# Edge pass of a graph network on one core: TensorE's segment sums move to the end of its step, and ScalarE's and VectorE's steps are put in another order

## The reference

```
gate = silu(edge_attr @ F1W + F1b) @ F2W + F2b          # 40 -> 48 -> 48, per edge
gate = gate + (emb[z[src]] * (emb[z[dst]] @ adapt)).sum(-1)
cw   = where(d < 6, 0.5 * (cos(pi * d / 6) + 1), 0)      # d: the edge's distance
msg  = gate * h[dst] * cw * node_mult[dst]
agg  = segment_sum(msg, src);  tot = segment_sum(node_mult[dst], src)
```

## Time and profile before

| what | before |
|---|---|
| three executions, median | 16926.92 us (16877.77 to 16951.38) |
| profiled execution, first to last instruction (its span; the record has no other time for it) | 19341.2 us |
| busy in it: TensorE, VectorE, GpSimd, ScalarE | 10354.6, 11255.4, 9389.6, 5378.0 us |
| edge pass, from its first transpose to its last eviction | 2577 to 6382 us |

### The profile page before, as it was taken

The page is one execution under the profiler, slowest core; times in us unless marked ns, Lnnn a source line. Parts: engine busy times, 40 slices in busy tenths (PEclk is TensorE's granted clock), DMA queues, the critical chain, the costliest instruction groups (busy, mean ns, idle before and its releaser), DMA issues. The chain is left out here.

```text
span 19341.2 us, 391384 instructions
## 1 busy us (share of the span) xinstructions
PE 10354.6 (54%) x115995; PEld 7977.8 (41%) x115995; DVE 11255.4 (58%) x26413; ACT 5378.0 (28%) x15471; POOL 9389.6 (49%) x11101
## 2 busy tenths in 40 slices
PE   1001046666666326884895787588355555543332
PEld 1001024444444116774784676477233333332332
DVE  6567034444444456885887688588533333347667
ACT  0000012222222003651563465266122222222221
POOL 7788654444444533441441343144254545538466
PEclk9755555555555559997997998799666666675665
DMA  4432334443435316554552754455211111152432
GB/s 130 143 86 64 96 73 73 73 74 73 74 73 72 49 31 226 160 143 141 171 161 63 238 161 124 172 162 161 57 38 45 41 45 41 43 170 60 115 113 49
DMA packets 1458569, 1976.55 MB, mean 102 GB/s; under 512 B 411908, under 2 KB 1125764, under 8 KB 1451465
## 3 DMA queue, kind: packets, MB, share of 16 engines
q1 hardware_dynamic: 1074622, 1326.66, 21.9%
q0 software_dynamic: 309216, 511.82, 14.6%
q10 hardware_dynamic: 74552, 135.95, 2.2%
HBM read 1245.74 MB, written 614.07 MB: 96 GB/s over the span
## 5 line engine op out<-in xcount | busy, mean ns | idle before, releaser
L681 POOL DMA_INDIRECT attend_rows<-key_rows,attend_fetch_now x1824 | 1754.4, 962 | 2354.8 <-PE attend_seg L1717 2026.0
L681 POOL DMA_INDIRECT edges_rows<-raw,edges_perm_now x1824 | 1765.3, 968 | 2006.2 <-issue 1631.5
L1761 ACT ACTIVATE attend_hot<-attend_lane_hot,attend_share 128x128 f32<-128x128 fp8e4 x7296 | 2227.1, 387 | 107.4 <-DVE attend_share L1784 73.5
L681 POOL DMA_INDIRECT mlp_xin<-table,mlp_staged x1564 | 1493.5, 955 | 1440.0 <-PEq L2308 979.9
L681 POOL DMA_INDIRECT keys_rows<-table,keys_staged x1564 | 1869.2, 1195 | 532.9 <-issue 532.9
L1717 PE MATMUL attend_seg<-attend_rows,attend_hot 128*128 128x49 f32 x14592 | 1847.3, 281 | 69.8 <-issue 38.9
L1717 PEld LDWEIGHTS attend_seg<-attend_rows,attend_hot 128*128 128x128 f32 x14592 | 1772.7, 198 | 109.6 <-issue 104.9
L681 POOL DMA_INDIRECT tally_rows<-rows_by_source,tally_origin_now x912 | 1210.9, 1328 | 297.4 <-issue 243.9
L1704 PE MATMUL attend_qx<-attend_table,attend_oht 128*128 128x90 bf16 x21888 | 1108.8, 209 | 445.5 <-DMA attend_oht<-src_hots 395.4
L1704 PEld LDWEIGHTS attend_qx<-attend_table,attend_oht 128*128 128x128 fp8e4 x21888 | 1011.7, 101 | 518.4 <-issue 516.6
L1801 DVE TENSOR_REDUCE attend_mraw<-attend_top 128x2 f32<-128x1024 f32 x912 | 1110.7, 1218 | 60.5 <-issue 30.7
(11 more groups left out here) (543 smaller groups left out, 23684.6 us busy)
## 6 DMA issues: line engine op xcount, KB each, us to landing
key_rows<-expand_out SPq DMA_DIRECT2D x304, 624.0 KB
attend_ea<-edge_attrs SPq DMA_DIRECT2D x912, 160.0 KB
attend_table<-q SPq DMA_DIRECT2D x1832, 67.5 KB
expand_oht<-dst_hots SPq DMA_DIRECT2D x304, 384.0 KB, 3.9
attend_oht<-src_hots SPq DMA_DIRECT2D x912, 128.0 KB
attend_lane_hot<-src_hots_by_edge SPq DMA_DIRECT2D x912, 128.0 KB
raw<-keys_rows ACTq DMA_DIRECT2D x46, 2176.0 KB
rows_by_source<-spread_out SPq DMA_DIRECT2D x152, 576.0 KB, 4.8
```

What stands on the lines that cost most here:

```text
L681: return nc.gpsimd.indirect_dma_start(out=out, out_offset=None, in_=table, in_offset=bass.IndirectOffsetOnAxis(ap=index, axis=0))
L1761: ins = nc.scalar.activation(hot[p][:, u, c, :], lane_hot8[r][:, u, c, :], ACT.Copy, scale=share[p][:, u, c:c + 1])
```

## The change

- TensorE: S moves from second place in the step to the last, behind A. The order becomes T, B, E, A, S.
- `val3` becomes two buffers, used in turn.
- ScalarE: step n now does the tables and the transposed attributes of chunk n-1, then the gate of chunk n-2, then the rows of chunk n, then silu and cosine of chunk n-1. The post that chunk n-1's rows are taken (`s_taken`) moves with the tables.
- VectorE: the eviction moves from the end of the step, for chunk n-2, to the place between the one-hots and the dot product, for chunk n-3. Its loop gets one more step at the end.

```diff
-        val3 = ph.sb("val3", [P, COL, 3, RW], BF16)
+        val3 = [ph.sb(f"val3{b}", [P, COL, 3, RW], BF16) for b in two]
 # TensorE: this block from behind T to behind A, with val3[p] for val3
-                if live(n, 2):
-                    pe.wait_ge(s_val, n - 1)
-                    after(pe, s_ev, n - 2)
...
+                if live(n, 2):
+                    pe.wait_ge(s_val, n - 1)
+                    after(pe, s_ev, n - 2)
...
 # ScalarE, the new step
+                if live(n, 1):
+                    act.wait_ge(s_dl, n)
+                    act.sem_inc(s_taken, 1)
+                    after(act, s_exp, n - 2)
+                    for u in range(CHR):
+                        block_i = act.value_load(k.irow[0:1, bass.ds((n - 1) * CHR + u, 1)], min_val=0, max_val=NT - 1)
+                        ins = a(table[1 - p][:, u], k.emb3[:, :, bass.ds(block_i * G, G)], ACT.Copy)
+                    ins.then_inc(s_table, 1)
+                    act.wait_ge(s_t, n)
+                    a(eT[:], ps_t[0:RBF], ACT.Copy).then_inc(s_tc, 1)
+                if live(n, 2):
+                    act.wait_ge(s_2, n - 1)
+                    a(gate[p][:], ps_2[:, 0:COL * F].rearrange("p (c f) -> p c f", f=F), ACT.Copy).then_inc(s_2c, 1)
                 if live(n, 0):
                     act.wait_ge(s_rows[b], (t + 1) * (16 * COL))
                     after(act, s_kept[p], halves(s, t) * 32)
+                    after(act, s_t, n - 1)
                     a(wt[p][:], rows[b][:, :, WT], ACT.Copy)
...
                 if live(n, 1):
+                    act.wait_ge(s_1, n)
                     a(act1[0:F], ps_1[0:F], ACT.Silu, bias=b1[:]).then_inc(s_1a, 1)
+                    after(act, s_seen, n - 2)
+                    act.wait_ge(s_arg, n)
+                    a(cw[1 - p][:], phase_[1 - p][:], ACT.Sin, bias=half[:], scale=-np.pi / 6.0).then_inc(s_cos, 1)
 # VectorE
+                if live(n, 3):
+                    dve.wait_ge(s_seg, n - 2)
+                    v.tensor_reduce(k.parts[:, bass.ds((n - 3) * (CHR * RW), CHR * RW)].rearrange("p (u w) -> p u w", u=CHR),
+                                    ps_s[:, 0:CHR * 3 * RW].rearrange("p (u j w) -> p u w j", u=CHR, j=3), AX, ALU.add).then_inc(s_ev, 1)
                 if live(n, 1):
                     r, o = rows[(s - 1) % TURN], 1 - p
                     dve.wait_ge(s_exp, n)
...
-                    after(dve, s_seg, n - 1)
+                    after(dve, s_seg, n - 2)
...
-                if live(n, 2):
-                    dve.wait_ge(s_seg, n - 1)
...
-            for s in range(2):
+            for s in range(3):
                 step(CHN + s, s, LOOPS)
```

More of the change, by code:

```diff
@@ L1121, in step @@
                     ins.then_inc(s_1, 1)
+                if live(n, 2):
+                    pe.wait_ge(s_val, n - 1)
+                    after(pe, s_ev, n - 2)
+                    pe.sem_inc(s_pe_turn, 1)
+                    for u in range(CHR):
+                        for c in range(GR):
+                            ins = mm(ps_s[:, u * (3 * RW):(u + 1) * (3 * RW)], hot_s8[p][:, u * GR + c, :], val3[p][:, u * GR + c].rearrange("p j w -> p (j w)"),
+                                     start=(c == 0), stop=(c == GR - 1))
+                    ins.then_inc(s_seg, 1)
             steps(pe, step, 2)
@@ L1131, in step @@
                 p, b = s % 2, s
-                st = n * CHR
+                if live(n, 1):
+                    act.wait_ge(s_dl, n)
+                    act.sem_inc(s_taken, 1)
+                    after(act, s_exp, n - 2)
+                    for u in range(CHR):
+                        block_i = act.value_load(k.irow[0:1, bass.ds((n - 1) * CHR + u, 1)], min_val=0, max_val=NT - 1)
[6 more added lines that the diff above has]
+                    a(gate[p][:], ps_2[:, 0:COL * F].rearrange("p (c f) -> p c f", f=F), ACT.Copy).then_inc(s_2c, 1)
                 if live(n, 0):
@@ L1138, in step @@
                     a(k.dl_a[:, bass.ds(n * COL, COL)], rows[b][:, :, DL], ACT.Copy).then_inc(s_dl, 1)
[L1139 to L1149, removed]
                 if live(n, 1):
[L1151 to L1154, removed]
+                    act.wait_ge(s_1, n)
                     a(act1[0:F], ps_1[0:F], ACT.Silu, bias=b1[:]).then_inc(s_1a, 1)
[L1156 to L1160, removed]
+                    after(act, s_seen, n - 2)
+                    act.wait_ge(s_arg, n)
+                    a(cw[1 - p][:], phase_[1 - p][:], ACT.Sin, bias=half[:], scale=-np.pi / 6.0).then_inc(s_cos, 1)
+            steps(act, step, 2)
         @block.vector
@@ L1223, in step @@
                     dve.sem_inc(s_seen, 1)
-                    split(v, ch, val[:], [val3[:, :, j, :] for j in range(3)], rest[:])
+                    split(v, ch, val[:], [val3[o][:, :, j, :] for j in range(3)], rest[:])
                     dve.sem_inc(s_val, 1)
-                if live(n, 2):
-                    dve.wait_ge(s_seg, n - 1)
-                    v.tensor_reduce(k.parts[:, bass.ds((n - 2) * (CHR * RW), CHR * RW)].rearrange("p (u w) -> p u w", u=CHR),
-                                    ps_s[:, 0:CHR * 3 * RW].rearrange("p (u j w) -> p u w j", u=CHR, j=3), AX, ALU.add).then_inc(s_ev, 1)
             for s in range(TURN):
```

## The result

The changed kernel takes 16724.6 us (median of 4 runs, 16703.8 to 16746.7) against 16920.9 (median of 4), 196 us between the two medians. The measured ratio is 0.9905, 95% interval 0.9883 to 0.9926: 161 us less, 125 to 198; the text goes by this ratio. Forecast were 420 less, 16507 in a range of 16310 to 16850. The sign was right and the time lies in the range, but the gain is 0.38 of the one forecast.

A forecast was written before the change was run, and what follows sets the result against it. TensorE's groups back to back, 10.94 us, were taken to bound the new step of 11.0; 12.9 - 11.0 = 1.9 us in 228 steps, 433 us, less 11 for lag, is 420 off 16926.9: 16507 us, range 16310 to 16850.

The forecast's parts named there:

- The hold comes with the recording: Edge pass: readers start 3.9 us after E ends; most of this delay comes with recording the trace, 75 in 100.
- S's own wait goes, S and T stand directly behind A and S: TensorE's step: S behind A no longer waits for VectorE; the next T finds its rows, 4.4 us to spare.
- The step before, without the hold: Edge pass of the kernel before: the ring of TensorE and ScalarE, 12.88 us, sets a step of 12.9 us.
- GpSimd's work, 10.2, a floor just under the new step: Edge pass: GpSimd's own work and a gap take 10.2 us a step, 0.8 under the new 11.0.
- VectorE's ring before, 12.60: Kernel before, late posts taken out: from E through dot product, eviction, S and B back to E, 12.60 us.
- new ring of 10.2: After the change: VectorE's cycle, with S, B and the eviction out of it, takes 10.2 us, 0.8 to spare.
- The second: Rival, 16 in 100: small gain, posts held until S has run or GpSimd stretching VectorE's ring to 12 us; about 16700.
- The first: Rival, 14 in 100: the hold is real in timed runs and ends with A; 536 us off, 16391.
- the fourth: Rival, 7 in 100: A's and E's posts are held until TensorE runs dry; 139 us slower, 17066.
- The third: Rival, 10 in 100: timed runs already have TensorE's upper clock, GpSimd's 10.2 us bounds both kernels; no change, 16927.
- The fifth: Rival, 3 in 100: TensorE's clock rises only after the change, the step falls to GpSimd's 10.2; 616 us off, 16311.
- The clock: TensorE in the edge pass: granted clock stays 0.50, 1.2 GHz, despite 9.1 us without a gap in every step.

The follow-up runs named there:

- the second recording: The kernel before, unchanged, recorded again: span 16882.7 us, step 11.92 us.
- the third of S: One of the three bf16 parts of the values kept in S: ratio to the kernel before 1.0010 in the kernel before, 0.9899 in the changed kernel.
- the order alone: ScalarE's new order put in the kernel before, with S in its old place and one val3 buffer: ratio 1.0087 to the kernel before.

## Why the prediction was wrong in size

- *The hold comes with the recording*: right, of that one recording; the second has none. What held the posts in it no run shows.
- *S's own wait goes, S and T stand directly behind A and S*: right where rows are there.
- ***The step before, without the hold*, 12.88: the step that failed.** It is 11.92. I took the hold out of the step but kept the group times that stood beside it, all at 0.50. In an undisturbed recording S often finds its values, follows T at once, and B and A of every second step run at 2.4 GHz. At 0.50 throughout the number was near (12.7 from the third of S, 12.66 with the order alone). The prediction had named this itself: wrong if the timed step was not near 12.9 before. This is 0.96 of the 1.15 us that the gain per step is short (1.9 forecast, 0.75 measured).
- *GpSimd's work, 10.2, a floor just under the new step*: 11.18. About half of the time of the gathers in the earlier trace rows, VectorE stood waiting for the held dot product (6.79 us); with both busy, 640 of 1576 gathers take over 1 us (156 of 1058 in the first recording). The new step is that row, 11.17 for 11.0. With the iota in PSUM it is 10.71.
- *VectorE's ring before, 12.60*: right at that clock; with the order alone it closes at 12.66. Its new ring of 10.2 was right as well, but not covered by TensorE's 10.94: where B runs at the upper clock it closes, at 10.27 from E to E in the median of the 67 steps of the changed kernel in which E waits, and at 10.43 with the operands in PSUM.
- *Rivals.* The second had the time, about 16700, from GpSimd and VectorE running side by side, but the wrong way round: the gathers are the ones stretched. The first and the fourth fall with the hold. The third had a piece of it: the upper clock is granted in timed runs, in the kernel before, for part of every second step. In the changed kernel it is granted too (0.55), but there GpSimd bounds and it buys nothing (0.9899 with a third of S, at 0.50). The fifth falls: the mean clock is no higher after the change, 0.55 for 0.57.
- *The clock*, 0.50 in the earlier trace rows: the second recording shows 0.92 in a stretch without gaps, which the held one hid. The Trainium skill, "TensorE: Matmul & The Clock Gate", section "The HAM clock gate", lets sustained activity release the throttle; that stretch agrees. Yet the changed kernel, nearly without gaps, has 0.55 over the pass, and with a third of S 0.50; what decides between them no run here shows.
- *The sum.* From its first transpose to its last eviction the pass takes 2790 us in the second recording of the kernel before and 2627 in the changed kernel: 163 less, all of it in the first 212 steps; the last 16 chunks take 259 in both. Measured: 161. That the time lies in the range is luck: the range was wide enough to take in three rivals, and of the two steps that were subtracted, 12.9 and 11.0, the first was 0.96 us too long.

## What to carry to other kernels

A disturbance that is taken out of a recording takes with it the clock and the overlaps that it made: record again before summing its rows, or bound the sum by both clock levels. An engine whose work in the trace lies in another's idle time has no proven floor; its time has to be taken from steps in which both are busy. And once gathers bound a loop, moving one operand of VectorE's long operations to PSUM can be worth over half as much again as the reordering that exposed them (103 us on top of 161), and three operands moved before it were worth nothing.

## What the runs showed of the hardware

A gather's instruction waits for a VectorE operation under way when both its inputs are in SBUF (0.61 us of 0.735 left at L1223, 0.37 of 0.494 at L878), also for the one-input L1201 from bf16 to fp8 (0.39 of 0.518); with one input in PSUM it does not (0.00 of 0.964), at the same length of the operation (1.21 for 1.22), and a gather that starts within about 0.02 us of the operation's start does not wait either (84 at L876). A recording of the profile can be 2.4 ms longer than the timed runs, with posts held for 3.9 us, and the next recording of the same kernel free of it. TensorE's clock can alternate from step to step in a steady loop, 10.2 and 13.7 us, and a kernel with less work can lose that: 0.57 to 0.50 with a third of S, with no time gained.
